# Routing in two halves, sigmoid rows stored before the choice of experts, and most of the slot tables and the shared expert moved into the expert loop

## The reference, cut to what matters

```python
x = L0_attn_q                                   # (2, 1024, 256) float32
xn = layernorm(x)
s = attention0(xn)                              # 16 heads, one key/value head of 128, head width 128
x = x + s * silu(ffn0(xn))
xn = layernorm(x)
s = attention1(xn)                              # causal over an axis of length 2
x = x + s * silu(ffn1(xn))                      # ternary weights, exact gelu

def ffn0(x):                                    # 2048 rows, 64 experts of width 88, 128 places in each
    scores = sigmoid(x @ router.T); sc = scores + e_bias
    group_scores = sum of the top 2 of sc in each of 8 groups of 8
    masked = sc where the group is among the best 4, else 0
    topk_idx = top 8 of masked
    topk_w = scores[topk_idx]; topk_w = topk_w / (topk_w.sum() + 1e-20) * 2.5
    # an expert takes its first 128 tokens, the others get nothing from it
    moe = sum over the 8 of  topk_w * ((silu(x @ w_gate[e]) * (x @ w_up[e])) @ w_down[e])
    return moe + (silu(x @ sh_gate) * (x @ sh_up)) @ sh_down     # the shared expert
```

## Time and profile before

| what | value |
|---|---|
| runs | 433.42, 434.67, 433.1 us |
| span of the profiled execution | 433.6 us |
| TensorE busy (matmul) | 348.9 us, 80% of the span |
| VectorE busy | 277.6 us, 64% |
| ScalarE busy | 197.5 us, 46% |
| GpSimd busy | 242.5 us, 56% |
| chain that ended last, by engine | PE 37%, DVE 24%, DMA 13%, issue 10%, ACT 7%, POOL 7% |
| DMA | 58.40 MB, mean 135 GB/s |

### The profile page before, as it was taken

How to read it: one execution, slowest core, us unless ns; L and a number is a source line. 1 busy time by engine, 2 the same in 40 slices (tenths; PEclk the granted TensorE clock), 3 DMA queues, 4 the chain that set the end, 5 groups by cost and what they waited for, 6 DMA issues and landing times.

```text
span 433.6 us, 6895 instructions
## 1 busy us (share of the span) xinstructions
PE 348.9 (80%) x2106; PEld 274.1 (63%) x2106; DVE 277.6 (64%) x826; ACT 197.5 (46%) x493; POOL 242.5 (56%) x230
## 2 busy tenths in 40 slices
PE   0899895878899896989799987967039889888894
PEld 0894354457688666868588775755027778777773
DVE  4928997185565452545556756554257888999875
ACT  1344351362454252474244444513017876766871
POOL 6460000537878867867888888846373346654211
PEclk9999998889999997999789999869658999999998
DMA  8770005897888788897767877544760000000001
GB/s 279 276 246 14 0 1 174 259 269 183 194 195 194 169 246 230 207 270 144 185 144 182 192 147 187 93 54 44 205 201 0 2 25 26 26 25 20 9 24 50
DMA packets 37703, 58.40 MB, mean 135 GB/s; under 512 B 6091, under 2 KB 27171, under 8 KB 37283
## 3 DMA queue, kind: packets, MB, share of 16 engines
q1 hardware_dynamic: 25379, 39.08, 28.0%
q0 software_dynamic: 12288, 18.88, 24.0%
HBM read 40.22 MB, written 17.73 MB: 134 GB/s over the span
## 4 chain that ended last, share of the span: by engine, by line
PE 37%; DVE 24%; DMA 13%; issue 10%; ACT 7%; POOL 7%; SPq 0%; POOLq 0%; DVEq 0%; ACTq 0%
DMA W<-tok_d,idxE 7%; PE two L1389 5%; PE two L1305 4%; PE two L1341 4%; DMA acc_d<-W,idxE 4%; PE two L1401 4%; PE two L1249 4%; DVE F L1128 3%; POOL ny L513 2%; PE two L1214 2%; PE two L1378 2%; PE two L1263 2%; PE two L1316 2%; ACT W L722 2%; ACT two L709 2%
## 5 line engine op out<-in xcount | busy, mean ns | idle before, releaser
L474 POOL DMA_INDIRECT acc_d<-W,idxE x64 | 103.7, 1621 | 33.4 <-DVE W L972 19.2
L454 POOL DMA_INDIRECT W<-tok_d,idxE x56 | 56.4, 1007 | 62.9 <-DMA tok_d<-F 46.1
L1008 DVE SCALAR_TENSOR_TENSOR W<-W,two 128x88 f32<-128x88 f32 x64 | 15.6, 244 | 63.2 <-ACT W L652 63.0
L636 ACT ACTIVATE W<-two 128x256 f32<-128x256 f32 x64 | 24.4, 382 | 49.9 <-PE two L1378 49.1
L1341 PE MATMUL two<-A,v 128*128 128x128 f32 x256 | 35.9, 300 | 5.5 <-issue 5.5
L1341 PEld LDWEIGHTS two<-A,v 128*128 128x128 f32 x256 | 35.1, 215 | 7.7 <-issue 6.9
L1508 PE MATMUL two<-W,A 128*128 128x257 f16 x256 | 29.9, 273 | 10.4 <-DVE F L1153 9.9
L1378 PE MATMUL two<-ident,W 128*128 128x128 f32 x112 | 23.2, 291 | 13.8 <-DMA W<-tok_d,idxE 11.7
L1508 PEld LDWEIGHTS two<-W,A 128*128 128x128 f16 x256 | 24.0, 98 | 15.9 <-DVE F L1153 11.7
L1475 PE MATMUL two<-F,wfcT 128*128 128x256 f16 x256 | 32.6, 282 | 1.4 <-DVE F L1091 1.4
L972 DVE TENSOR_SCALAR W<-two,W 128x256 f32<-128x256 f32 x56 | 26.8, 479 | 10.0 <-PE two L1401 7.0
(11 more groups left out here) (221 smaller groups left out, 830.3 us busy)
## 6 DMA issues: line engine op xcount, KB each, us to landing
W<-in_gu SPq DMA_DIRECT2D x20, 352.0 KB
F<-in_gu SPq DMA_DIRECT2D x12, 352.0 KB
acc_d<-xn SPq DMA_DIRECT2D x8, 512.0 KB, 4.4
W<-in_dn SPq DMA_DIRECT2D x20, 176.0 KB
F<-in_dn SPq DMA_DIRECT2D x12, 176.0 KB
x<-in_q SPq DMA_DIRECT2D x4, 512.0 KB, 6.9
A<-in_Wo SPq DMA_DIRECT2D x1, 2048.0 KB, 13.1
tok_d<-xn SPq DMA_DIRECT2D x4, 512.0 KB, 4.3
```

The costliest lines, as they stand in the source:

```text
L454: pool.indirect_dma_start(out=xg[n % XR], out_offset=None, in_=tok_d[:, :], in_offset=bass.IndirectOffsetOnAxis(ap=idxE[:, n:n + 1], axis=0))\
L474: pool.indirect_dma_start(out=acc_d[n % 2][:, :], out_offset=bass.IndirectOffsetOnAxis(ap=idxE[:, n:n + 1], axis=0), in_=ysb[n % YS], in_o ...
L636: sc.activation(xgT[n % 2], bk_(2)[:, 0:D].rearrange("p (k n) -> p k n", k=KH), ACT.Copy)\
```

## The change

- **Normalisation.** ScalarE, not VectorE, writes xn for tiles 0 to 11; the inverse roots of chunks 1 to 3 come from a power on GpSimd (`root`) and a Newton step on VectorE. TensorE starts when the identity matrix is ready and no longer when all constants are.
- **Routing in halves.** `route(0)` runs on tiles 0 to 7, `route(1)` on 8 to 15. It works on tanh + (2 bias + 1), twice the score; ScalarE makes the sigmoids beside it. xn and the sigmoids are one tile `xr` of 320 columns, stored in two halves as soon as they are there, and nothing of the weights' sum is needed for that.
- **Weights' sum at the end.** `put` multiplies by the sigmoid alone. The sum is applied to the accumulated rows: half of 2.5/sum is the scale of the tanh in `gate` and 2.5/sum is multiplied into the attention's output. The shared output is multiplied by sum/2.5 within the loop (`shared_weighed`) and added in the tail.
- **Tables.** Groups of 16 experts: group 0 ahead of the loop, groups 1 to 3 within it.
- **Shared expert.** Only `shared_up(0)` and its product stay ahead of the loop. The rest is at experts 1 to 8.
- **Accumulators** are zeroed by two DMAs out of a zeroed stretch of SBUF, issued early, and no longer wait for the shared expert.
- **Tail.** The first pair's total, product and sum move to VectorE; GpSimd's `total` has a second add for the other pairs; `gate` is two instructions.

The new numbers of the schedule and the core of the diff:

```diff
+DOWN_AT = {1: (0, 0), 2: (0, 1), 3: (1, 0), 4: (1, 1), 5: (2, 0), 6: (2, 1), 7: (3, 0), 8: (3, 1)}
+UP_AT = {1: 1, 3: 2, 5: 3}
+PRODUCT_AT = {2: 1, 4: 2, 6: 3}
+HOT_AT = {0: (1, 0), 1: (1, 1), 2: (1, 2), 3: (1, 3), 9: (2, 0), 10: (2, 1), 11: (2, 2), 13: (2, 3),
+          19: (3, 0), 20: (3, 1), 21: (3, 2), 23: (3, 3)}
+NUMBER_AT = {1: (1, 0), 2: (1, 1), 10: (2, 0), 11: (2, 1), 20: (3, 0), 21: (3, 1)}
+SLOTS_AT, SPREAD_AT, TURN_AT, TAKE_AT = 4, 5, 6, 7
+SLOTS_TILE = {2: 2, 5: 3}
+TURN_TILE = {3: 2, 6: 3}
+DEN_AT, WEIGH_AT = 8, (12, 14, 16, 18)
...
+            def clear(i):
+                sp.dma_start(acc_d[i].rearrange("(p t) d -> p (t d)", p=P).rearrange("p (r z) -> p r z", z=ZW0),
+                             zero.unsqueeze(1).to_broadcast([P, (NTOK + P) * D // P // ZW0, ZW0])).then_inc(acc_init, 16)
...
+            sp.wait_ge(zero_ready, 1)
+            clear(0)
+            for h in range(2):
+                xn_wait(sp, HT * h + HT)
+                sp.wait_ge(sig_ready, h + 1)
+                sp.dma_start(tok_v[:, HT * h:HT * h + HT, :], xr[:, HT * h:HT * h + HT, :]).then_inc(xn_stored, 16)
...
+            load_experts(0)
+            load_experts(1)
+            clear(1)
+            for g in range(2, WR):
                 load_experts(g)
...
+            def root(c):
+                cols = slice(4 * c, 4 * c + 4)
+                pool.wait_ge(ln1_var, c + 1)
+                pool.tensor_tensor(rstd[:, cols], lnv[:, cols], expo[:, 0:4], ALU.pow).then_inc(ln1_pow, 1)
...
             pool.wait_ge(idxE_ready, 1)
-            pool.wait_ge(xn_stored, 5 * 16)
-            pool.wait_ge(w_stored, 2 * 16)
+            pool.wait_ge(xn_stored, 3 * 16)
...
-            pool.wait_ge(acc_init, 10 * 16)
+            pool.wait_ge(acc_init, 2 * 16)
...
-                pool.tensor_tensor(pair(xn, p), pair(xn, p), pair(acc1, p), ALU.add).then_inc(acc_ready, 1)
+                then(pool.tensor_tensor(pair(tot, p), pair(tot, p), pair(acc1, p), ALU.add))
+                pool.tensor_tensor(pair(tot, p), pair(tot, p), pair(xn, p), ALU.add).then_inc(acc_ready, 1)
...
+            norm(0)
+            norm(1)
+            for t in range(NT):
+                take_xT(t)
+                if t + 2 < LN_ACT:
+                    norm(t + 2)
+                if t == HT:
+                    take_tanh(0)
+                if t == HT + 2:
+                    sigmoid(0)
+            take_tanh(1)
...
+            route(0)
+            route(1)
+            select(0, 1)
...
+                then(ve.scalar_tensor_tensor(out=s0[:, u, :], in0=bk_(1)[:, 0:D], scalar=rinv[:, t:t + 1], in1=bo_b,
+                                             op0=ALU.mult, op1=ALU.add))
+                ve.tensor_scalar(s0[:, u, :], s0[:, u, :], rden[:, u:u + 1], None, ALU.mult).then_inc(s0_ready, 1)
...
             ve.wait_ge(pos_ps, 1)
+            then(ve.tensor_copy(v_i[:, 0], pos(0).rearrange("p (e t) -> p t e", t=NT)))
             masks(0)
+            hot_high(0)
+            hot_low(0, SB)
             number(0)
-            then(ve.scalar_tensor_tensor(out=s_w, in0=s_rep, scalar=BIG / 2, in1=s_sig, op0=ALU.is_ge, op1=ALU.mult))
...
-            ve.tensor_tensor(s_w, s_w, rden[:, :].unsqueeze(2).to_broadcast([P, NT, NE]), ALU.mult).then_inc(w_ready, 1)
             spread_slots(0)
             take_indices(0)
+            select(1, NG)
...
+            def first_total():
+                ve.wait_ge(acc_ld[0], 32)
+                then(ve.tensor_tensor(pair(tot, 0), pair(tot, 0), pair(acc1, 0), ALU.add))
+                ve.tensor_tensor(pair(tot, 0), pair(tot, 0), pair(xn, 0), ALU.add).then_inc(tot_first, 1)
+                ve.wait_ge(tot_first, 1)
+                then(ve.tensor_tensor(pair(s0, 0), pair(s0, 0), pair(tot, 0), ALU.mult))
...
+            keys(0)
+            values(0)
+            keys(1)
+            values(1)
+            turn_v(0)
+            keys(2)
+            pe.wait_ge(sel_ready, 1)
+            pe.wait_ge(tanh_ready, 2)
+            positions(0, 1).then_inc(pos_ps, 1)
+            values(2)
+            turn_v(1)
+            keys(3)
+            values(3)
+            turn_v(2)
+            pe.wait_ge(kv_ready, 8)
+            slots(0)
+            indices(0)
+            turn_v(3)
             pe.wait_ge(ld_sh, 2 * 16)
+            shared_up(0)
+            pe.wait_ge(sel_ready, 2)
             pe.wait_ge(v_ready, 4)
-            shared_up(0)
-            positions()
-            shared_up(1)
-            shared_down(0)
-            shared_up(2)
+            positions(1, 2)
+            positions(2, 4).then_inc(pos_ps, 1)
...
+                if n in DOWN_AT:
+                    if n == 1:
+                        pe.wait_ge(pos_act, 2)
+                    shared_down(*DOWN_AT[n])
+                if n in UP_AT:
+                    shared_up(UP_AT[n])
+                if n == SLOTS_AT:
+                    slots(1)
+                if n == TURN_AT:
+                    indices(1)
```

More of the change, by code:

```diff
@@ L135, in build @@
         rstd = sb("rstd", [P, NT])
+        nmr, lnt = [sb(n, [P, NT]) for n in ("nmr", "lnt")]
         gsum = sb("gsum", [P, 2])
@@ L967, in put, with shared_weighed @@
+            def shared_weighed(t0, t1):
+                ve.wait_ge(sy_ready, NT // 2)
+                for t in range(t0, t1):
+                    last = mark(ve.tensor_scalar(xn[:, t, :], xn[:, t, :], den[:, t:t + 1], None, ALU.mult))
+                ve.wait_ge(dve, last)
             def put(n):
@@ L1240, in turn_v, with keys, values @@
                 ins.then_inc(vt_ps, 1)
+            def keys(c):
+                if c >= 2:
+                    pe.wait_ge(kv_ready, 2 * (c - 1) - 1)
+                for k in range(KH):
+                    ins = pe.matmul(bk_(4 + 2 * (c % 2)), Wk_s[:, k, :], xT[:, 4 * c:4 * c + 4, k, :], start=(k == 0),
+                                    stop=(k == KH - 1))
+                ins.then_inc(kv_ps, 1)
+            def values(c):
+                if c >= 2:
+                    pe.wait_ge(kv_ready, 2 * (c - 1))
+                for k in range(KH):
+                    ins = pe.matmul(bk_(5 + 2 * (c % 2)), Wv_s[:, k, :], xT[:, 4 * c:4 * c + 4, k, :], start=(k == 0),
+                                    stop=(k == KH - 1))
+                ins.then_inc(kv_ps, 1)
@@ new lines, in shared_up, with shared_down @@
+            def shared_up(c):
+                if c:
+                    pe.wait_ge(shT_ready, c)
+                for m in range(2):
+                    for k in range(KH):
+                        ins = pe.matmul(bk_(4 + m)[0:FF, :], sgu[:, m, k, :], xT[:, SC * c:SC * c + SC, k, :], start=(k == 0),
+                                        stop=(k == KH - 1))
+                ins.then_inc(sgu_ps, 1)
+            def shared_down(c, j):
+                pe.wait_ge(shT_ready, c + 1)
+                if 2 * c + j:
+                    pe.wait_ge(sy_ready, 2 * c + j)
+                for i in range(2):
+                    at = P * (2 * j + i)
+                    ins = pe.matmul(bk_(0)[:, D * i:D * i + D], sh_h[c % 2][:, at:at + P], sdn, start=True,
+                                    stop=True)
+                ins.then_inc(sdn_ps, 1)
@@ new lines, in positions, with slots @@
+            def positions(g0, g1):
+                es = slice(GE * g0, GE * g1)
+                out_ = bk_(0) if g1 - g0 == 2 else pos(g0)
+                pe.matmul(out_, before16[:, :], sel16[:, es, :].rearrange("p e t -> p (e t)"), start=True, stop=False)
+                return pe.matmul(out_, ones16[:, :], cum16[:, es, :].rearrange("p e t -> p (e t)"), start=False, stop=True)
+            def slots(g):
+                pe.wait_ge(hot_ready, g + 1)
+                pe.wait_ge(tid_ready, ACT_T * (g + 1))
+                for t in range(NT):
+                    ins = pe.matmul(slot_out(g), hot_a[:, t].rearrange("p a e -> p (a e)"), hot_b[:, :, t, :],
+                                    start=(t == 0), stop=(t == NT - 1))
+                ins.then_inc(slot_ps, 1)
@@ L1412, in _ @@
                     turn_h(n - 1)
-                if n in SLOTS_AT:
-                    slots(1, SLOTS_AT.index(n))
-                if n == TURN_AT:
-                    indices(1)
                 if n == SUM_AT:
```

613 lines of the change are left out of this document (306 added, 307 removed).

## The result

The changed kernel took 429.51 us (427.62 to 431.49, 4 runs) beside 433.26 us (433.05 to 434.67, 4 runs) for the kernel before: ratio 0.990, 95% interval 0.985 to 0.995. In a second comparison it took 428.40 beside 434.87: 0.984 (0.9815 to 0.987). So it is faster by 1.0 to 1.6%; by the medians that is 3.8 and 6.5 us. The forecast was 9.6 us. The profiled execution is the longest of the first four, 431.49 us with a span of 429.8. In every execution with both on record the time is 1.7 us more than the span. So the span of 433.6 that the prediction set out from answers to a time of about 435.3 and not, as it says, to the median of 433.42. Both profiles lie 2.0 above their medians, and the difference of 3.8 is the same either way.

The account below looks back on a forecast made before the run. It took the head's chain through TensorE and VectorE's routing, GpSimd in the loop and GpSimd's power in the tail as limits. -23.8 + 11.6 + 3 - 0.4 = -9.6 from 433.6 gave 424.0 us; eight-in-ten range 413 to 432.

Parts of the forecast that it names:

- Start: Head up to the loop's first turning on TensorE: at 62 instead of 85.77, 23.8 us earlier.
- the hold: Head: GpSimd's adds for WoS beside route(0) stretch VectorE's instructions; cost 3.5 us, bounds 0 and 5.6.
- rival 1: Head: the adds don't hold the routing, first turning at 58.5; total 420.5 us, chance 0.20.
- rival 3: Head: full hold of 5.6 us and 3 for the clock, first turning at 66; total 428.0, chance 0.15.
- slots start 8.0 after the selection: Head: slots wait for last keys, values and ScalarE's copies; index list 0 at 57.5, with 1.2 us for the clock.
- Experts 0 to 8: Loop's first turning to scatter 7: 43.0 us instead of 31.4, giving back 11.6; scatter 7 at 105.0.
- Rival 4: Experts 0 to 8: TensorE at half level through the shared work adds 19 us; total 443, chance 0.08.
- Rest of the loop: From scatter 7 on: tables, weighing and in-order waits add 3 us, bounds -2 and +12.
- GpSimd's floor: Loop: scatter, gather and two gaps take 3.18 us an expert, 178.1 of 185.3; most added VectorE work is beneath it.
- Tail: After the last scatter: first power 2.6 us earlier, five periods 2.2 longer; net -0.4, bounds -2.6 and +4.
- the first power at 314.8: Tail: GpSimd, without pair 0, has its first power at 314.8 instead of 317.41, 2.6 us earlier.
- power and all behind it are 0.45 late in each of five periods: Tail: each total is longer by 1.27 us and a wait, against 0.96 idle; +2.2 in all.

Follow-up runs that it names:

- run 2: Changed kernel with 2 of GpSimd's 15 adds for WoS done, the others left out: 425.13 us, ratio 0.9795 to the kernel before.
- Run 11: Changed kernel with keys, values and turnings ahead of the positions, except the last chunk's values, and ScalarE's copies ahead of numbering: 426.44 us, ratio 0.982.
- the five profiles: Two profiles of the changed kernel and those of runs 1, 6 and 10, same code up to the tail: loop from scatter 7 187.1 to 190.5 us.
- run 5: Kernel before with one more GpSimd add over a pair between total and gated, result unused: 440.31 us beside 436.03, ratio 1.008.
- run 4: Changed kernel with tables, slots and index lists made for groups 0 and 1 only, copied for 2 and 3: 425.52 us, ratio 0.981.
- run 10: Changed kernel with GpSimd's powers ahead of its product, which waits for VectorE's scales behind the Newton step: 425.43 us, ratio 0.976.
- run 1: Changed kernel with GpSimd's product put behind the power in the tail: ratio 0.999 to the kernel before, powers 14.01 us apart.
- run 13: Changed kernel with the edits of Run 11 and run 10 together: 425.71 us, ratio 0.978 to the kernel before.
- run 6: Changed kernel with the third norm's mean square and variance reading one input from PSUM, in four single-element instructions: 427.15 us, ratio 0.9785.

## Why the prediction was wrong

Forecast -9.6, measured -3.8, then -6.5. The time lies in the range, the direction was right, the size was not.

*Start: mechanism right, 2 short.* The first tile came at 9.99 (9.8), route(0) at 21.1 (21.0), the hold cost 4.1 (3.5), as the rows of one-input normalisations had suggested, and so neither nothing (rival 1) nor 5.6 (rival 3); run 2 shows that it is the adds. A half of the routing without a hold took 10.0 and not 9.6. Not all instructions are held: L909 took 0.21 between two that took 0.70 and 0.75. For the rest, the prediction let slots start 8.0 after the selection and add 1.2 for the clock. They started 9.7 after it: half level fell on the values (3.62), and ScalarE numbered the table (3.0) ahead of copying them. Run 11 has the list at 55.5.

*Experts 0 to 8: right within 2.* 41.0 us from the first turning to scatter 7 for a forecast of 43.0, at a granted clock of 0.98; 1 of the 2 is what had been added for half level, the other has no cause shown. (The prediction's 34.3 us of work has nine experts at 13.4, which by its own terms are 13.8; that is small.) Rival 4 is refuted: no half level to speak of over the shared work.

*Rest of the loop: mechanism right, size within its scatter.* +3 was forecast and +1.8 to +5.2 came in the five profiles, against the one of the kernel before; against run 5's loop (184.0), which has the same code, it is 1.3 more. The tables are the greater part of it (run 4), and at one of their stops the in-order list is seen. The prediction took GpSimd's floor for a cover that hides most of 23 us of VectorE's work; it hides most, and by run 4 lets 3.7 to 7.1 through.

*Tail: this step failed*, in two terms, 3.7 in all. The larger is "the first power at 314.8", 12.3 after the last scatter; it came 15.10 after it (2.8). VectorE's part was nearly right: without two holds its variance would be there 12.8 after (L1165 lasts 1.79 where its neighbours of the same size last 0.69, L1191 1.25 for 0.17). I had freed GpSimd of pair 0 and forgotten that pair 1 stands ahead of the power in its list: its rows let GpSimd start 10.7 after the last scatter, its two adds and the product run until 15.0 after, and hold VectorE meanwhile. With the product behind the power it is 13.96, 14.96 and 14.88 (runs 10, 1 and 13). The product's part is then gone, but the two adds still hold L1165 (1.63), and in runs 1 and 13 the instruction before it as well (1.78 and 1.37 for 0.69). No run takes the adds away, so that 12.8 would be reached is not shown. The smaller term is "power and all behind it are 0.45 late in each of five periods" (2.2); in four periods it is 0.68 each (2.7), and the tail behind the first power is 3.1 longer in all, 0.9 more than forecast. I had counted GpSimd's third instruction as a delay of GpSimd alone. Before, the product ended ahead of the square; pushed back by 1.35 it lies on the square, and the variance, not GpSimd, is late. Run 5 makes this period out of the old one by that instruction alone, run 6 removes the hold and keeps the lateness (13.36), runs 10 and 13 remove both (12.95).

The Trainium skill, "SBUF — State Buffer", section "SBUF: two separate sides", has the rule that decides here, and the prediction weighed it for the head alone: VectorE with two SBUF inputs and a GpSimd instruction that reads SBUF exclude each other for a whole instruction. Runs 1, 5, 6 and 10 agree: 0.90 to 1.23 with two SBUF inputs, and two instructions in 0.22 with one of the inputs in PSUM, beside the same product. L1191, one float32 input of two elements, is held as well (1.25); no run here separates why.

The tail's +3.3 is within the bounds I had put on it (-2.6 and +4). What was wrong is that I took the value near the good end, although pair 1 stands ahead of the power in GpSimd's list.

## What to carry to other kernels

A GpSimd instruction that is added or moved is to be laid over VectorE's list by time: the price is not its own length on GpSimd but what small VectorE instruction of the critical chain it then covers, above all one with two SBUF inputs: here such an instruction lasted until GpSimd's ended (0.90 for 0.16, 1.23 for 0.17). Moving it away by order alone can move it onto a dearer one (run 1); let it wait for a semaphore behind the chain's last small two-input instruction (run 10, and the period of run 13). Where engine time is taken as hidden below another engine's floor, look for the places where the in-order lists are long and the bounding engine has no lead.

## What was not expected of the hardware

- A square of two elements a partition lasts as long as its neighbour on GpSimd lets it: 0.16 or 0.90 us; a 6-element product 0.17 or 1.23.
- The same instructions after the same idle time (3.59 and 3.60 us) ran at full level in one execution (1.91) and at half level in another (3.47), with slightly different pauses further back. The Trainium skill, "TensorE: Matmul & The Clock Gate", section "What's actually happening", says that the count of slow matmuls differs from run to run of the same kernel; the same code at two levels agrees. Here that is worth 1.6 us in the head and 1.15 in one period of a tail. The executions of one kernel lie 3 to 6 us apart, and this can be one part of it; for the loop's share (187.1 to 190.5) no single cause was found.
